# A list scheduler's cross-engine latency raised from 520 to 580 in a transformer-layer kernel

## The chip, the cores and the metric

The kernel runs on all 8 cores of one Trainium2 chip. Each core computes one of 8 sequences of 4096 tokens by itself; no data passes between cores. The metric is the device time of the slowest core in microseconds (us), the median of several runs. A matmul engine instruction is written PE, the vector engine DVE, the scalar engine ACT, GpSimd POOL, and SyncE SP.

## The reference, cut to what matters

The layer is linear attention with rotary embedding followed by a matrix product with the signs of a weight, both behind a layer norm and with a residual. D is 1024, there are 16 heads of 64.

```python
x = x + attn(layernorm(x), Wq, Wk, Wv, Wo)
x = x + einsum('bsi,oi->bso', layernorm(x), sign(weight))

# attn, per head:
q, k = phi(rope(x @ Wq.T)), phi(rope(x @ Wk.T)); v = x @ Wv.T      # phi(x) = elu(x) + 1
# scan over tokens t:
K_sum += k_t;  KV += outer(k_t, v_t)
y_t = (q_t @ KV) / max(q_t . K_sum, 1e-6)
# all heads' y side by side, then @ Wo.T
```

## The kernel before, in words

A core works through its sequence in 32 chunks of 128 tokens. The scan is done by chunk: inside a chunk a masked 128x128 product per head (L596, masked by DVE at L602 into Asb), between chunks a running sum kv in PSUM (L610) that ACT copies to KVs (L619 to L623). Each chunk has a front part (layer norm, transposes into ln1T, the products with wq, wk, wv, rope and phi, transposes into qT and kT) and a back part (attention, product with wo, residual x2, second layer norm, product with wf, residual, store). The loop at L716 mixes the back of chunk c with the front of chunk c+1.

Every product with a weight is `emit_proj` (L463): 64 matmuls of 128x128 with a sum over eight, the first 32 into one PSUM bank, the last 32 into another. When a bank is complete, it is read by ACT (qev and kev at L484, vaug at L555) or by DVE (x2 at L680 after wo, outb at L696 after wf). The banks att, pjA, pjB and pjC are handed out in turn, so the names in a row change from chunk to chunk. Of wo's two banks the one with the first half of the columns is called bank 0 here, the other bank 1. DVE adds the residual from bank 0 first (one L680), then from bank 1 (the other L680). All transposes of a chunk share one PSUM tile, ptr: L422 (ln1 and ln2), L437 (qphi, kphi) and L660 (Ysb, whose copy by ACT, L668, is the YT that wo multiplies).

No order is written by hand. Every instruction is recorded with an estimated cost and the instructions it depends on; `schedule` then runs a list scheduling for all engines, and each engine executes its instructions in the order that comes out, with semaphore waits where the data come from another engine. Two places in `schedule` use the constant `LAT`: the priority of an instruction is its cost plus the longest path behind it, with `LAT` for each edge (L80), and an instruction on another engine may start `LAT` after its producer ends (L111). An instruction is picked by earliest start, then priority (L99).

Of the kernel before, what the change touches and what calls it, by code (L numbers as in the profile page):

```python
# [28 lines left out]
class Sched:  # L29
# [34 lines left out]
    def schedule(self):  # L64
        ops = self.ops
        n = len(ops)
        succ = [[] for _ in range(n)]
        pend = [0] * n
        for op in ops:
            for d in op["deps"]:  # L70
                succ[d].append(op["i"])
                pend[op["i"]] += 1
        LAT = float(os.environ.get("SIMLAT", 520.0))
        prio = [0.0] * n
        for i in range(n - 1, -1, -1):
            m = 0.0
            for sj in succ[i]:
                if prio[sj] > m:
                    m = prio[sj]
            prio[i] = ops[i]["cost"] + (LAT if succ[i] else 0.0) + m  # L80
        eng_free = {e: 0.0 for e in ENGINES}
        avail = [0.0] * n
        done = [0.0] * n
        ready = {e: [] for e in ENGINES}
        for i in range(n):
            if pend[i] == 0:
                ready[ops[i]["engine"]].append(i)
        order = []
        remaining = n
        while remaining:  # L90
            best = None
            for e in ENGINES:
                lst = ready[e]
                if not lst:
                    continue
                ef = eng_free[e]
                for i in lst:
                    st = ef if ef > avail[i] else avail[i]
                    key = (st, -prio[i], i)  # L99
                    if best is None or key < best[0]:  # L100
                        best = (key, e, i)
            key, e, i = best
            st = key[0]
            ready[e].remove(i)
            done[i] = st + ops[i]["cost"]
            eng_free[e] = done[i]
            order.append(i)
            remaining -= 1
            for sj in succ[i]:
                pend[sj] -= 1  # L110
                t = done[i] + (LAT if ops[sj]["engine"] != e else 0.0)  # L111
                if avail[sj] < t:
                    avail[sj] = t
                if pend[sj] == 0:
                    ready[ops[sj]["engine"]].append(sj)
        cnt = {e: 0 for e in ENGINES}
        for i in order:
            ops[i]["eidx"] = cnt[ops[i]["engine"]]
            cnt[ops[i]["engine"]] += 1
        self.sim_makespan = max(done) if n else 0.0  # L120
        if os.environ.get('SIM_PRINT'):
            print('SIM makespan:', round(self.sim_makespan / 1000, 1), 'us')
            start_t = {i: done[i] - ops[i]["cost"] for i in range(n)}
            eng_prev = {}
            last = {e: None for e in ENGINES}
            for i in order:
                e2 = ops[i]["engine"]
                eng_prev[i] = last[e2]
                last[e2] = i
            cur = max(range(n), key=lambda i: done[i])  # L130
            from collections import Counter
            hist = Counter(); hist_t = Counter()
            while cur is not None:
                st = start_t[cur]
                nxt = None
                for d in ops[cur]["deps"]:
                    t = done[d] + (LAT if ops[d]["engine"] != ops[cur]["engine"] else 0)
                    if abs(t - st) < 1e-6:
                        nxt = d
                        break  # L140
                if nxt is None:
                    ep = eng_prev[cur]
                    if ep is not None and abs(done[ep] - st) < 1e-6:
                        nxt = ep
                import re as _re
                key = _re.sub(r"\d+", "#", ops[cur]["tag"]) or ops[cur]["engine"]
                hist[key] += 1; hist_t[key] += ops[cur]["cost"]
                cur = nxt
            print("SIM critical-path composition (count, total_us):")
            for k, v in hist.most_common(16):  # L150
                print(f"  {k:24s} n={v:5d}  t={hist_t[k]/1000:.1f}us")
        return order
# [666 lines left out]
```

How the kernel before makes its waits and increments, by code:

```python
        def emit_engine(name, eng):  # L744
            for op in by_engine[name]:
                i = op["i"]
                for (kind, tgt, val) in waits[i]:
                    if kind == "dma":
                        eng.wait_ge(dsems[tgt], 16 * val)
                    else:
                        eng.wait_ge(sems[tgt], inc_no[val])
                instr = op["fn"](eng)
                if op["dma"]:
                    k = dma_no[op["i"]]
                    instr.then_inc(dsems[(name, (k - 1) % 3)], 16)
                elif needs_inc[i] and instr is not None:
                    instr.then_inc(sems[name], 1)
            if name in ("sync", "gpsimd"):
                nq = sum(1 for op in by_engine[name] if op["dma"])
                for j in range(3):
                    m_tot = (nq - j + 2) // 3
                    if m_tot > 0:
                        eng.wait_ge(dsems[(name, j)], 16 * m_tot)
```

## Time and profile before

| what | value |
|---|---|
| median of 3 runs | 1180.21 us (1179.9 to 1181.19) |
| profiled execution, its own time | 1181.88 us |
| profiled execution, span of its slowest core | 1180.2 us |
| spans of the 8 cores | 1174.7 to 1180.2 us |
| PE, busy in the span | 885.2 us (75%) |
| DVE, busy | 664.0 us (56%) |
| ACT, busy | 536.0 us (45%) |
| POOL, busy | 159.2 us (13%) |
| DMA, mean | 40 GB/s |

The profile comes from one execution, and its rows are of the slowest core unless another is named. The span runs from the first to the last instruction of that core; the execution's own time is 1.7 us more. No engine is busy throughout: the shares say that the engines wait for each other.
### The profile page before, as it was taken

How to read it: one execution, taken by the hardware profiler on the slowest of the kernel's cores; microseconds unless marked ns; L12 is line 12 of the kernel's file. 1: busy time of each engine (PE TensorE's matmuls, PEld its weight loads, DVE VectorE, ACT ScalarE, POOL GpSimd, SP SyncE). 2: the span in 40 equal slices, each digit the busy share in tenths (PEclk: the TensorE clock that was granted, in tenths of full speed). 3: DMA queues.
4: the chain of work that ended last, by engine and by line, in shares of the span. 5: the costliest groups of instructions: out<-in, count | busy, mean ns of one | idle time of the engine just before them, and what ended most of it. 6: DMA issues, size and time to landing. Idle time of an engine off the chain costs nothing.

```text
span 1180.2 us, 33759 instructions; the slowest of 8 cores (1174.7 to 1180.2 us)
## 1 busy us (share of the span) xinstructions
PE 885.2 (75%) x13571; PEld 811.7 (69%) x13571; DVE 664.0 (56%) x1322; ACT 536.0 (45%) x1183; POOL 159.2 (13%) x139
## 2 busy tenths in 40 slices
PE   2427887788877877887787787878777888787785
PEld 1427776677777766777776677777667777776675
DVE  5134555665555566655556665555566555556652
ACT  3125444545444455454444545444454554445441
POOL 1201100111110011111011111110011111011110
PEclk9758899999999999999999999999999999999996
DMA  9890100110011011101101110110011101101000
GB/s 166 127 137 19 38 28 28 38 37 31 26 37 37 20 38 37 37 20 38 37 20 38 37 38 19 38 37 32 25 37 38 37 20 38 37 20 37 20 20 19
DMA packets 15145, 46.78 MB, mean 40 GB/s; under 512 B 1424, under 2 KB 1424, under 8 KB 14992
## 3 DMA queue, kind: packets, MB, share of 16 engines
q1 hardware_dynamic: 9504, 33.62, 7.8%
q0 software_dynamic: 5488, 11.01, 6.2%
q8 instruction: 109, 1.79, 0.6%
q14 instruction: 44, 0.36, 0.1%
HBM read 38.86 MB, written 16.78 MB: 47 GB/s over the span
## 4 chain that ended last, share of the span: by engine, by line
PE 29%; issue 23%; DVE 23%; ACT 12%; DMA 7%; POOL 3%; DVEq 1%; ACTq 0%; POOLq 0%; SPq 0%
PE att L470 6%; PE pjA L470 6%; PE pjC L470 6%; PE pjB L470 6%; DVE x L680 4%; DVE junkV L380 4%; DVE Asb L602 4%; POOL rB L502 3%; DMA wk<-wkT 3%; ACT qT L449 3%; ACT kev L484 2%; PE ptr L422 2%; DMA wf<-wfT 2%; DVE outb L696 2%; PE ptr L437 2%
## 5 line engine op out<-in xcount | busy, mean ns | idle before, releaser
L500 POOL TENSOR_TENSOR rA<-qev,tabS_s 128x512 bf16<-128x512 bf16 x32 | 37.0, 1158 | 835.8 <-ACT qev L484 742.7
L470 PE MATMUL pjC<-wo,YT 128*128 128x128 bf16 x480 | 83.0, 252 | 25.1 <-ACT YT L668 25.1
L470 PE MATMUL att<-wo,YT 128*128 128x128 bf16 x544 | 94.9, 255 | 7.4 <-ACT YT L668 7.4
L470 PE MATMUL pjA<-wo,YT 128*128 128x128 bf16 x544 | 94.0, 254 | 6.6 <-ACT YT L668 6.6
L470 PE MATMUL att<-wv,ln1T 128*128 128x128 bf16 x512 | 71.4, 223 | 20.3 <-ACT kev L484 13.2
L470 PE MATMUL pjB<-wo,YT 128*128 128x128 bf16 x480 | 82.3, 251 | 5.7 <-ACT YT L668 5.7
L470 PE MATMUL pjA<-wv,ln1T 128*128 128x128 bf16 x512 | 71.0, 222 | 15.4 <-ACT kev L484 15.4
L470 PE MATMUL pjC<-wv,ln1T 128*128 128x128 bf16 x512 | 70.6, 219 | 15.6 <-ACT kev L484 15.6
L470 PE MATMUL pjB<-wv,ln1T 128*128 128x128 bf16 x512 | 70.2, 219 | 15.0 <-ACT kev L484 15.0
L470 PE MATMUL pjB<-wf,ln2T 128*128 128x128 bf16 x512 | 78.1, 223 | 2.1 <-ACT ln2T L428 2.1
L470 PE MATMUL pjC<-wf,ln2T 128*128 128x128 bf16 x512 | 77.3, 223 | 1.6 <-ACT ln2T L428 1.6
L470 PE MATMUL pjA<-wf,ln2T 128*128 128x128 bf16 x512 | 77.4, 219 | 1.4 <-ACT ln2T L428 1.4
L470 PE MATMUL att<-wf,ln2T 128*128 128x128 bf16 x512 | 77.0, 219 | 1.3 <-ACT ln2T L428 1.3
L470 PE MATMUL att<-wq,ln1T 128*128 128x128 bf16 x512 | 72.4, 223 | 6.5 <-DMA wq<-wqT 6.5
L619 ACT CAST KVs<-kv 64x455 bf16<-64x455 f32 x31 | 16.5, 533 | 127.1 <-PE kv L610 127.1
L470 PE MATMUL pjA<-wq,ln1T 128*128 128x128 bf16 x512 | 72.5, 224 | 0.0
L470 PEld LDWEIGHTS pjC<-wo,YT 128*128 128x128 bf16 x480 | 52.9, 116 | 26.1 <-issue 26.1
L470 PE MATMUL pjB<-wq,ln1T 128*128 128x128 bf16 x512 | 70.3, 220 | 0.0
L470 PE MATMUL pjC<-wq,ln1T 128*128 128x128 bf16 x512 | 70.0, 219 | 0.0
L680 DVE TENSOR_TENSOR x<-pjC,xs 128x512 f32<-128x512 f32 x15 | 10.4, 692 | 104.2 <-PE pjC L470 103.0
L422 PE MATMUL ptr<-ident_s,ln 128*128 128x128 bf16 x512 | 53.7, 267 | 19.3 <-DVE ln L415 18.9
L470 PEld LDWEIGHTS att<-wo,YT 128*128 128x128 bf16 x544 | 60.9, 118 | 8.6 <-issue 8.6
(152 smaller groups left out, 2987.3 us busy)
## 6 DMA issues: line engine op xcount, KB each, us to landing
xs<-x SPq DMA_DIRECT2D x32, 512.0 KB, 3.9
out<-outb SPq DMA_DIRECT2D x32, 512.0 KB, 2.6
wq<-wqT POOLq DMA_DIRECT2D x1, 2048.0 KB, 21.9
wk<-wkT POOLq DMA_DIRECT2D x1, 2048.0 KB, 34.2
wv<-wvT POOLq DMA_DIRECT2D x1, 2048.0 KB, 47.2
wo<-woT POOLq DMA_DIRECT2D x1, 2048.0 KB, 19.4
wf<-wfT POOLq DMA_DIRECT2D x1, 2048.0 KB, 26.7
tabS_s<-tabS POOLq DMA_DIRECT2D x1, 256.0 KB, 27.9
```

The costliest lines, as they stand in the source:

```text
L380: s.add("vector", lambda e: e.tensor_scalar(out=junkV[sti][:], in0=x_sb[:], scalar1=-1.0 / D, scalar2=0.0, op0=ALU.mult, op1=ALU.add, accu ...
L422: s.add("tensor", lambda e, i=i: e.transpose(ptr[:, i * 128:(i + 1) * 128], src_sb[:, i * 128:(i + 1) * 128], ident[:]), reads=[src_res, " ...
L437: s.add("tensor", lambda e, i=i: e.transpose(ptr[:, i * 128:(i + 1) * 128], src_sb[:, i * 128:(i + 1) * 128], ident[:]), reads=[src_res, " ...
L449: s.add("scalar", lambda e, a0=a0, a1=a1: e.copy(dv[:, a0:a1, 0, :], pv[0:64, a0:a1, :]), reads=[rres], writes=[wres], tag=f"ev_{tag}e{hb} ...
L470: s.add("tensor", lambda e, o=o, i=i, pj=pj, off=off, lsb=lsb, w_sb=w_sb: e.matmul(pj[:, off:off + 128], lsb[:, i * 128:(i + 1) * 128], w_ ...
L484: s.add("scalar", lambda e, half=half, pj=pj, dst_sb=dst_sb: e.copy(dst_sb[:, half * 512:(half + 1) * 512], pj[:]), reads=[pjres], writes= ...
L500: s.add("gpsimd", lambda e: e.tensor_tensor(out=rAv, in0=HI, in1=Sb, op=ALU.mult), reads=[src_res, "tabS"], writes=["rA"], tag=f"{tag}_rA")
L502: s.add("gpsimd", lambda e: e.tensor_tensor(out=rBv, in0=LO, in1=Sb, op=ALU.mult), reads=[src_res, "tabS"], writes=["rB"], tag=f"{tag}_rB")
L602: s.add("vector", lambda e, g=g, ab=ab: e.tensor_tensor(out=Asb[:, g * 512:(g + 1) * 512].rearrange("p (h t) -> p h t", t=128), in0=ab[:, ...
L619: s.add("scalar", lambda e, kvv=kvv: e.copy(kvv[0:64, 0:455], kv[0][0:64, :]), reads=["kv0"], writes=[kvres_w], tag=f"kvev{c}_0", cost=550)
L680: s.add("vector", lambda e, half=half, pj=pj, x2sb=x2sb, x_sb=x_sb: e.tensor_tensor(out=x2sb[:, half * 512:(half + 1) * 512], in0=pj[:], i ...
L696: s.add("vector", lambda e, half=half, pj=pj, osb=osb, x2sb=x2sb: e.tensor_tensor(out=osb[:, half * 512:(half + 1) * 512], in0=pj[:], in1= ...
```

## The change

One number: the latency between engines that the scheduler reckons with goes from 520 to 580 ns.

```diff
-        LAT = float(os.environ.get("SIMLAT", 520.0))
+        LAT = float(os.environ.get("SIMLAT", 580.0))
```

The instructions are the same, and on DVE, ACT, POOL and SP they stand in the same order. Only PE's order differs, and no PE instruction moves far. The chunks in the middle of the program are alike, apart from the names of the banks, in either kernel, so one chunk shows what moved. Three places follow.

PE, the end of wo's product, where wk begins (in this chunk wo's bank 0 is pjB and bank 1 is pjC). Before:

```order
L470 MATMUL pjC<-wo,YT 128x128
L470 MATMUL pjB<-wo,YT 128x128
L470 MATMUL pjC<-wo,YT 128x128 x3
L470 MATMUL att<-wk,ln1T 128x128 x13
L470 MATMUL pjA<-wk,ln1T 128x128 x11
```

With the change:

```order
L470 MATMUL pjC<-wo,YT 128x128
L470 MATMUL pjB<-wo,YT 128x128
L470 MATMUL pjC<-wo,YT 128x128 x2
L470 MATMUL att<-wk,ln1T 128x128 x13
L470 MATMUL pjA<-wk,ln1T 128x128 x11
```

The last matmul into pjB had three matmuls into pjC behind it and has two now: bank 0 is complete one matmul later, bank 1 where it was. Between the same two neighbours (the YT transposes and wk) stand the same 136 instructions: wo, wq and the eight ln1 transposes. The last wq matmul into its first bank stays in its place, the one into its second bank moves two places ahead.

PE, around the transposes of kphi in the same chunk (the banks pjB and pjC hold wf's product here, att and pjA wv's). Before:

```order
L470 MATMUL pjB<-wf,ln2T 128x128
L470 MATMUL pjC<-wf,ln2T 128x128
L437 MATMUL ptr<-ident_s,kphi 128x128 x8
L470 MATMUL att<-wv,ln1T 128x128
L470 MATMUL pjA<-wv,ln1T 128x128
L470 MATMUL pjC<-wf,ln2T 128x128
```

With the change:

```order
L470 MATMUL pjB<-wf,ln2T 128x128
L470 MATMUL pjC<-wf,ln2T 128x128
L470 MATMUL att<-wv,ln1T 128x128
L470 MATMUL pjA<-wv,ln1T 128x128
L437 MATMUL ptr<-ident_s,kphi 128x128 x8
L470 MATMUL pjC<-wf,ln2T 128x128
```

Two wv matmuls that stood behind the eight transposes stand ahead of them. Behind the transposes 11 matmuls are left before the attention products L596, where there were 13.

PE, the same transposes in the two chunks before the last (here att and pjA hold wf's product, pjB and pjC wv's). Before:

```order
L437 MATMUL ptr<-ident_s,kphi 128x128 x7
L470 MATMUL pjB<-wv,ln1T 128x128
L470 MATMUL pjC<-wv,ln1T 128x128
L470 MATMUL att<-wf,ln2T 128x128
L470 MATMUL pjA<-wf,ln2T 128x128
L437 MATMUL ptr<-ident_s,kphi 128x128
```

With the change:

```order
L437 MATMUL ptr<-ident_s,kphi 128x128 x7
L470 MATMUL pjA<-wf,ln2T 128x128
L437 MATMUL ptr<-ident_s,kphi 128x128
```

Between the seventh transpose and the eighth stands one matmul in place of four; the other three are ahead of the first transpose.

Smaller moves, once in each chunk: the ln2 transposes come one place earlier (7 wv matmuls ahead of them, were 8), and three kv matmuls (L610) stand ahead of the first L633 where there were two, and seven at the end where there were eight. In the first chunk's front, 44 wq matmuls stand ahead of wk's first 23, where it was 46 and 25. In the last chunk, wf's product ends as wo's does: two matmuls into bank 1 behind the last into bank 0, where there were three.

## Rows read from the trace of the kernel before

**Rows 1.** The page: busy time of PE, and the chain that ended last by engine.
```profile
PE 885.2 (75%) x13571; PEld 811.7 (69%) x13571; DVE 664.0 (56%) x1322; ACT 536.0 (45%) x1183; POOL 159.2 (13%) x139
...
PE 29%; issue 23%; DVE 23%; ACT 12%; DMA 7%; POOL 3%; DVEq 1%; ACTq 0%; POOLq 0%; SPq 0%
```
**Rows 2.** Timeline of DVE, one chunk: start us, duration us, what [idle before it <-releaser].
```profile
617.32 0.69 DVE L680 TENSOR_TENSOR x<-pjB,xs 128x512 f32<-128x512 f32 x1 [10.45 <-PE pjB L470]
618.18 0.69 DVE L680 TENSOR_TENSOR x<-pjC,xs 128x512 f32<-128x512 f32 x1 [0.17 <-DVE x L680]
...
632.96 0.42 DVE L456 COPY kT<-ptr 64x512 bf16<-64x512 bf16 x1 [0.97 <-PE ptr L437]
...
633.93 0.69 DVE L696 TENSOR_TENSOR outb<-pjC,x 128x512 f32<-128x512 f32 x1
```
**Rows 3.** Timeline of PE, the same chunk.
```profile
616.99 0.22 PE L470 MATMUL pjB<-wo,YT 128*128 128x128 bf16 x1
617.04 0.33 PE L470 MATMUL pjC<-wo,YT 128*128 128x128 bf16 x3
...
632.24 0.61 PE L437 MATMUL ptr<-ident_s,kphi 128*128 128x128 bf16 x8 [1.19 <-ACT qT L452]
...
633.25 0.33 PE L470 MATMUL pjA<-wv,ln1T 128*128 128x128 bf16 x3
```
**Rows 4.** Timeline of ACT, the same chunk.
```profile
616.30 0.59 ACT L484 CAST qev<-att 128x512 bf16<-128x512 f32 x1 [5.22 <-PE att L470]
617.02 0.59 ACT L484 CAST qev<-pjA 128x512 bf16<-128x512 f32 x1
...
631.03 1.07 ACT L452 COPY qT<-ptr 64x512 bf16<-64x512 bf16 x2
```
**Rows 5.** Stretches by engine: busy us (instructions), then PEclk, DMA share, GB/s.
```profile
604.50:607.90 3.40, 1.29 (x16) 0.77 (x16) 1.95 (x7) 1.91 (x5) 0.00 (x0) 1.00 0.02 5
607.95:611.30 3.35, 3.25 (x31) 3.28 (x32) 0.00 (x0) 1.52 (x3) 0.00 (x0) 0.50 0.00 0
611.40:617.20 5.80, 5.80 (x107) 5.80 (x105) 0.00 (x0) 0.76 (x2) 0.00 (x0) 1.00 0.01 3
...
93.90:99.30 5.40, 5.38 (x51) 5.40 (x52) 0.00 (x0) 1.43 (x3) 0.00 (x0) 0.50 0.01 3
1120.60:1123.30 2.70, 2.70 (x26) 2.70 (x27) 0.00 (x0) 1.09 (x3) 0.00 (x0) 0.50 0.00 0
```
**Rows 6.** Timeline of PE, three chunks: the matmul in which the clock rises.
```profile
133.46 0.26 PE L470 MATMUL att<-wo,YT 128*128 128x128 bf16 x1
...
611.30 0.26 PE L470 MATMUL pjC<-wo,YT 128*128 128x128 bf16 x1
...
1089.13 0.28 PE L470 MATMUL att<-wo,YT 128*128 128x128 bf16 x1
```
**Rows 7.** Timeline of ACT and DVE: YT's copy in two chunks, the first residual add.
```profile
93.19 1.06 ACT L668 COPY YT<-ptr 128x512 bf16<-128x512 bf16 x2
...
607.32 1.07 ACT L668 COPY YT<-ptr 128x512 bf16<-128x512 bf16 x2 [0.99 <-PE ptr L660]
...
104.20 0.69 DVE L680 TENSOR_TENSOR x<-pjC,xs 128x512 f32<-128x512 f32 x1 [30.01 <-PE pjC L470]
```
**Rows 8.** Span and mean granted clock of two of the cores.
```profile
core 4: 1174.7 us, clock 0.926
core 5: 1180.2 us, clock 0.921
```
**Rows 9.** Timeline of PE, kphi's transposes in the second chunk before the last.
```profile
1109.98 0.55 PE L437 MATMUL ptr<-ident_s,kphi 128*128 128x128 bf16 x7 [1.19 <-ACT qT L452]
...
1110.59 0.22 PE L437 MATMUL ptr<-ident_s,kphi 128*128 128x128 bf16 x1
```
**Rows 10.** Timeline of DVE and ACT before the first wo.
```profile
53.33 1.37 DVE L504 TENSOR_TENSOR rC<-qev,tabC_s 128x512 bf16<-128x512 bf16 x1 [28.68 <-DMA tabC_s<-tabC]
...
85.49 7.03 ACT L326 ACTIVATE wf<-wf 128x8192 bf16<-128x8192 bf16 x1 [17.35 <-DMA wf<-wfT]
```

## The prediction
> **What bounds the kernel now.** I read the page first: PE is busy 75% of the span, and the chain that ended last is shared out between PE, issue time, DVE and ACT [rows 1]. So no engine sets the time; a ring of waits does, and what counts is where an instruction of the ring moves. The timeline of one chunk shows the ring. DVE sits idle for 10.45 us until wo's bank 0 is complete (its last matmul starts at 616.99), then does the first residual add at 617.32; the second add follows 0.86 later, not because of bank 1, whose last three matmuls began at 617.04, but behind the first add [rows 2, 3]. From there layer norm, rope and phi run in DVE's order, ACT copies qT until 632.10, PE does kphi's transposes at 632.24 after 1.19 us of waiting, DVE copies kT from 632.96, and masks and divides without a pause worth naming until the next YT [rows 2 to 4]. Then PE has 136 instructions in a row (wo, wq, ln1's transposes), and the ring closes.
>
> The second thing to see is TensorE's clock. Between 604.5 and 607.9 PE is busy for 1.29 of 3.40 us while DVE divides; after that the granted clock is 0.50 (1.2 GHz) from 607.95 to 611.30, while PE works at wo, and 1.00 (2.4 GHz) from 611.4 on [rows 5]. The start-to-start distance is 3.35/31 = 0.108 us in the slow stretch and 0.054 to 0.056 in the fast one [rows 3, 5]; I use 0.107 and 0.056. The rises are the point: the matmuls that straddle them stand at 133.46, 611.30 and 1089.13 [rows 6], 14 chunks apart each, and (1089.13 - 133.46)/28 = 34.13 us, (611.30 - 133.46)/14 = 34.13. Does the rise follow the work, or the work the rise? In the first chunk YT is copied at 93.19, and the rise (one period before 133.5) is at 99.4, 6.2 later; at 607.32 the distance is 4.0 [rows 5 to 7]. So it is not a fixed time after the work starts. From YT to the first add it takes 104.20 - 93.19 = 11.01 us in the one and 617.32 - 607.32 = 10.00 in the other [rows 2, 7]. 2.2 us more distance cost 1.0 us, a slope of 0.46, which is what the two rates give: a matmul done slow costs 0.107 in place of 0.056, so (0.107 - 0.056)/0.107 = 0.48 per us. That makes a lock: if the ring gets later by s against the rise, more of wo is done fast, and only 0.52 s of the delay is left at the first add. The ring's period is then the rises' 34.13 us, whatever small amount the ring itself gains or loses.
>
> Here a rule of the skill bears on it: the Trainium skill, "TensorE: Matmul & The Clock Gate", section "What's actually happening", says that the monitor's intervals run freely and are not restarted by a kernel, so that what varies is where in them a burst of matmuls falls. By that rule the rises keep their places under this change and the locked sum below holds; were the rise tied to the start of the burst instead, the unlocked sum of the rivals would. The equal distances of the rises [rows 6] beside unequal distances from YT [rows 7] agree with the rule.
>
> **The change, part by part.**
> - Bank 0 of wo is complete one matmul later, in each of 32 chunks. It lies on the path: DVE waits for it. The 136 instructions between the YT transposes and wk are the same, and by the end of wo the clock is fast, so the add starts 0.056 later than it would. With the lock, the shift at the first add in chunk n is s(n) = 0.52 s(n-1) + 0.056, which settles at 0.056/0.48 = 0.117 us after some five chunks and does not grow. Without the lock it would be 32 x 0.056 = 1.79 us.
> - wq's second bank is complete two places earlier. Nothing: the second qev copy starts 0.72 after the first [rows 4], behind it, and the first hasn't moved.
> - ln2's transposes one place earlier, kv matmuls in another order: hidden. They stand where DVE masks and divides back to back; cover gone, one place costs 0.056 a chunk, and the lock would eat that as well.
> - kphi's transposes two places later in 29 chunks. Hidden on both sides: PE has waited 1.19 us there for ACT [rows 3], which holds 2 x 0.056 = 0.11 with ease. Nor is the shorter tail behind them a gain: the tail's last matmuls start at 633.25 and end by 633.6, while outb's second half, which needs it, is taken up by DVE at 633.93 behind the kT copies [rows 2, 3].
> - kphi's transposes in two late chunks. The eight started at 1109.98 after the same wait, and the eighth came at 1110.59, 11 places later [rows 9]. With the change it is 8 places behind, and DVE's first kT copy waits for it: 3 x 0.056 = 0.167 us earlier, twice, on the path.
> - The start. DVE's first rope instruction waits for a table until 53.33, and the first wo stands behind ACT's sign of wf, which waits for its load and takes 7.03 us from 85.49 [rows 10]. Two wq matmuls moved near 40 us reach neither: 0. Were they on the path they would cost about 2 x 0.107 = 0.2.
>
> The sum, on the profiled execution: +0.117 at the first add of chunk 30; minus 0.167 at the kphi transposes makes -0.050; the next add 0.52 x -0.050 + 0.056 = +0.030; minus 0.167 makes -0.137; the last chunk's add -0.071 + 0.056 = -0.015; wf's bank 0, also one matmul later, 0.52 x -0.015 + 0.056 = +0.05 us. The last wf matmuls run as wo's do, slow first and then fast. So 1181.88 becomes 1181.9. The median of the runs is 1180.21, 1.7 below the profiled execution; the same step there gives 1180.3. That the runs differ by 1.3 us, and cores 4 and 5 by 5.5 [rows 8], with one program, I put down to where the rises fall for each; the change moves none of them.
>
> **The rivals.**
> - No lock: each chunk passes its 0.056 on. 1.79 + 0.06 for the last wf bank - 0.33 = +1.5, so 1181.7. For it: the row of DVE's wait ends on exactly this matmul. Against it: the slope of 0.46. A price of the skill would make it dearer: "TensorE: Matmul & The Clock Gate", section "Back-to-back issue gap", gives some 81 ns for each sustained matmul of 128 columns, which would make this case an estimated 33 x 0.081 - 6 x 0.081 = +2.2 us; rows 3 and 5 have 54 to 56 ns, and they decide.
> - A missed rise, the case on the slower side. The lock makes the ring start 0.12 us later against the rise. The slow part of wo is 5.4 us long in the first chunk, about 3.35 in the middle, and 2.7 near the end [rows 5]; where it starts too late for one rise, the core gets a later one. The place is wo's start in an early chunk or the one at 1120.6, where it starts latest. The price, from the longest and the shortest of these rows, is 5.4 - 2.7 = 2.7 us, which stays because the ring then hangs on the later rises: 1180.3 + 2.7 = 1183.0. It decides once the slowest core's slow part must be less than 2.7; a shift of 0.12 hardly goes there, and late in the program the 0.167 gained works against it.
> - The shorter tail counts: if the outb and vaug copies behind the kphi transposes set the pace, 2 x 0.056 x 29 = 3.2 us are saved: 1177.0. Against it stand the 0.3 us between the tail's end and DVE's taking it up [rows 2, 3], and the lock, which would give 0.1 back at most.
>
> **How the numbers follow.** A measurement of this kernel tells about 0.2%, 2.4 us, from no change. The locked case has 0.78 and its own range is that of the runs before, widened a little: 1179.2 to 1181.7. No lock has 0.11, and it too stays within 0.2%. A missed rise has 0.07, the shorter tail 0.04. Faster by over 0.2%: 0.04, and 0.01 for what I don't see. Slower: 0.07 and 0.01. Within: 0.87. The range takes in the first two cases and stops short of the other two: 1178.9 to 1182.2.
>
> **What would show it.** In the changed kernel's trace, rises 34.13 us apart as before; in a middle chunk YT's copy about 0.11 us nearer to the rise (3.9 in place of 4.0 us), and YT to first add still near 10.0; only two matmuls into bank 1 behind the last into bank 0, and the add 0.33 us after the start of that last one; PE's wait at kphi's transposes near 1.1 us in place of 1.19. Wrong would be: chunks 34.19 us apart, which means no lock; a slow stretch of wo longer than in the chunk before it, in mid program, which means a missed rise; DVE's kT copies starting sooner after ACT's qT copies, which means a gain that I have called hidden.

## The result and the profile after

The changed kernel takes 1191.64 us, the median of 8 runs from 1191.08 to 1192.75; the kernel before took 1181.3 in the same measurement. The ratio is 1.009, with a 95% interval of 1.0079 to 1.0102: slower by 0.9%, where I had forecast no change (1180.3) and a range up to 1182.2. The profiled execution of the changed kernel took 1191.08. In a few executions, whichever the kernel, the cores of a die run at a lower granted clock and take over 1% longer (one of the eight of before, 1197.05 us); the ratios leave these out, the medians count them.

The page of the changed kernel, with its line of busy times, the granted clock in 40 slices, and the chain that ended last:

```profile
PE 896.9 (75%) x13571; PEld 821.6 (69%) x13571; DVE 665.0 (56%) x1322; ACT 535.9 (45%) x1183; POOL 159.3 (13%) x139
...
PEclk9858997899999998989999999999979899999996
...
PE 31%; DVE 23%; issue 22%; ACT 12%; DMA 7%; POOL 3%; DVEq 1%; ACTq 0%; POOLq 0%; SPq 0%
```

Against [rows 1] the same number of matmuls keeps PE busy for 11.7 us more, while DVE and ACT are where they were. PE's own matmuls have become longer, which a lower clock does. The mean granted clock is lower on every core, but the cores don't lose alike; two of them, with span and mean granted clock:

```profile
core 4: 1189.4 us, clock 0.907
core 5: 1180.1 us, clock 0.914
```

Core 5 is where it was and core 4 is 14.7 us longer [rows 8]. Over the eight cores the mean span goes from 1177.3 to 1185.6, +8.4. A loss that one core has in full and another hardly at all isn't a fixed price per chunk. So I looked for the chunks in which core 4 loses it. These are the stretches of core 4 between the changes of its granted clock, with the last 3.3 us ahead of a fall cut off as a row of its own (busy us and instructions of PE, PEld, DVE, ACT, POOL; then PEclk, DMA share, GB/s):

```profile
439.70:443.00 3.30, 2.90 (x28) 2.93 (x29) 0.00 (x0) 1.69 (x4) 0.00 (x0) 0.50 0.02 5
443.10:463.50 20.40, 17.68 (x307) 17.03 (x304) 12.79 (x23) 11.16 (x28) 4.73 (x4) 1.00 0.09 28
463.60:466.90 3.30, 1.60 (x23) 1.33 (x24) 2.20 (x5) 1.81 (x4) 0.00 (x0) 1.00 0.00 0
467.00:480.50 13.50, 11.98 (x120) 10.22 (x120) 5.50 (x15) 3.47 (x7) 0.00 (x0) 0.50 0.10 40
480.70:501.00 20.30, 17.01 (x294) 16.29 (x293) 13.22 (x23) 11.86 (x28) 4.82 (x4) 1.00 0.09 29
501.10:504.40 3.30, 1.90 (x29) 1.37 (x25) 3.03 (x7) 1.18 (x2) 0.00 (x0) 1.00 0.23 96
504.60:514.60 10.00, 8.76 (x91) 7.49 (x92) 3.96 (x12) 3.47 (x7) 0.00 (x0) 0.50 0.04 15
514.80:545.40 30.60, 23.35 (x387) 21.09 (x384) 20.31 (x41) 15.02 (x35) 4.82 (x4) 1.00 0.10 36
```

The first row is the normal slow stretch at wo's start, and the last a normal fast one, which lasts until the next wo. Between them the clock falls early twice. It falls at 467.0, in the middle of attention and not at wo, and stays at 0.50 (1.2 GHz) for 13.65 us, through the division and most of the next wo. A chunk later it falls at 504.5 for 10.2 us, and then the rhythm is back. The rises stand at 443.06, 480.61 and 514.74, 37.55 and 34.13 apart. So this episode has moved the ring from one rise to a later one, and has cost 37.55 - 34.13 = 3.42 us for good.

Core 4 of the kernel before, the same part of a chunk in its own rhythm (it rises at 469.39):

```profile
469.40:489.80 20.40, 17.67 (x304) 16.91 (x302) 12.87 (x23) 11.40 (x28) 4.81 (x4) 1.00 0.09 29
489.90:493.20 3.30, 1.98 (x29) 1.67 (x29) 2.11 (x5) 1.54 (x3) 0.00 (x0) 1.00 0.00 0
493.30:500.00 6.70, 4.26 (x65) 3.14 (x64) 5.14 (x14) 1.78 (x4) 0.00 (x0) 1.00 0.19 78
500.20:503.50 3.30, 3.22 (x31) 3.25 (x32) 0.00 (x0) 1.50 (x3) 0.00 (x0) 0.50 0.02 5
```

What PE did in the 3.3 us from about 20.5 us after the rise differs: 1.98 us busy with 29 matmuls before, where the clock held, and 1.60 us with 23 after, where it fell. The timeline of PE shows what is missing. Core 4 after the change, from kphi's transposes to the second group of attention products:

```profile
464.38 0.61 PE L437 MATMUL ptr<-ident_s,kphi 128*128 128x128 bf16 x8 [1.08 <-ACT qT L452]
...
465.27 0.33 PE L470 MATMUL att<-wv,ln1T 128*128 128x128 bf16 x3
466.19 0.38 PE L596 MATMUL pjA<-qT,kT 96*128 96x128 bf16 x4 [0.58 <-DVE kT L459]
466.91 0.47 PE L596 MATMUL pjB<-qT,kT 96*128 96x128 bf16 x3 [0.34 <-DVE outb L696]
```

The same before the change:

```profile
490.41 0.61 PE L437 MATMUL ptr<-ident_s,kphi 128*128 128x128 bf16 x8 [1.19 <-ACT qT L452]
...
491.41 0.33 PE L470 MATMUL pjA<-wv,ln1T 128*128 128x128 bf16 x3
492.21 0.38 PE L596 MATMUL pjB<-qT,kT 96*128 96x128 bf16 x4 [0.47 <-DVE kT L459]
492.94 0.38 PE L596 MATMUL pjC<-qT,kT 96*128 96x128 bf16 x4 [0.34 <-DVE outb L696]
```

The wait for ACT is 0.11 shorter and the one for DVE's kT is 0.11 longer: two matmuls have crossed from behind the first wait to ahead of it, and no wait is longer in sum. The stretch between is poorer by them, and the chunk also stands later against the clock: the transposes start 464.38 - 443.06 = 21.32 us after the rise, against 490.41 - 469.39 = 21.02.

Counted in the clock records of all eight cores between 100 and 1100 us, the kernel before has no slow stretch over 11 us, and the changed one has 19 of 13.65 us, called early falls from here on: one to four on each core, five of them between 464 and 467 us. Each comes with a second, of 10.2 us, in the next chunk. (A lone slow stretch of 10.2 us near 120 us, after which the rises stand where they would, is not counted: the kernel before has it on two cores, the changed one on four.) 19 x 3.42 / 8 = 8.1 us for a mean core, of the +8.4 found. In the 19 chunks where an episode begins, kphi's transposes start 21.17 to 21.35 us after the rise, and none of the 190 other chunks whose clock held until the division has them later than 21.16. The kernel before has 17 chunks that stand as late, 21.17 to 21.33, and its clock holds in all of them; its median is 20.95. So neither the late place nor the moved transposes are enough alone: an early fall takes both.

### The profile page after: what moved, and what is told of

It reads as the page before. It is cut to its first block, busy times and chain, and to the rows that moved or that the text cites. A ratio compares the mean times of both kernels' runs of the same rounds, so it can differ in the third digit from the quotient of the medians.

```text
span 1189.4 us, 33759 instructions; the slowest of 8 cores (1180.1 to 1189.4 us)
## 1 busy us (share of the span) xinstructions
PE 896.9 (75%) x13571; PEld 821.6 (69%) x13571; DVE 665.0 (56%) x1322; ACT 535.9 (45%) x1183; POOL 159.3 (13%) x139
## 4 chain that ended last, share of the span: by engine, by line
PE 31%; DVE 23%; issue 22%; ACT 12%; DMA 7%; POOL 3%; DVEq 1%; ACTq 0%; POOLq 0%; SPq 0%
PE att L470 6%; PE pjC L470 6%; PE pjA L470 6%; PE pjB L470 6%; DVE x L680 4%; DVE junkV L380 4%; DVE Asb L602 3%; POOL rB L502 3%; DMA wk<-wkT 3%; ACT qT L449 3%; ACT kev L484 3%; PE ptr L422 2%; DMA wf<-wfT 2%; DVE outb L696 2%; PE ptr L437 2%
## 5 line engine op out<-in xcount | busy, mean ns | idle before, releaser
L470 PE MATMUL pjC<-wo,YT 128*128 128x128 bf16 x480 | 87.3, 258 | 24.6 <-ACT YT L668 24.6
L470 PE MATMUL att<-wo,YT 128*128 128x128 bf16 x544 | 97.6, 257 | 7.4 <-ACT YT L668 7.4
L470 PE MATMUL pjB<-wo,YT 128*128 128x128 bf16 x480 | 85.6, 255 | 5.8 <-ACT YT L668 5.8
L470 PEld LDWEIGHTS pjC<-wo,YT 128*128 128x128 bf16 x480 | 55.6, 119 | 25.7 <-issue 25.7
L470 PEld LDWEIGHTS pjA<-wo,YT 128*128 128x128 bf16 x544 | 62.2, 117 | 7.5 <-issue 7.5
L470 PE MATMUL pjB<-wq,ln1T 128*128 128x128 bf16 x512 | 67.4, 219 | 0.0
```

Of the source, the lines that this page charges most:

```text
L470: s.add("tensor", lambda e, o=o, i=i, pj=pj, off=off, lsb=lsb, w_sb=w_sb: e.matmul(pj[:, off:off + 128], lsb[:, i * 128:(i + 1) * 128], w_ ...
```

## The experiments

The kernels e1 to e4 have PE's order of before (LAT 520) with some of the pieces taken from the order at 580; `arrange` puts them together, and its letters name the pieces: K kphi's transposes, W the stretch of wo and wq, L ln2's transposes, V the kv matmuls, S the first chunk, F the last wf. The other engines' orders are the same in both.

**e1: kphi's transposes alone.**

```diff
-        order = s.schedule()
+        order = arrange(s, "K", None)
```

> PE's order as before, with only kphi's transposes where the change puts them (two wv matmuls ahead of them that stood behind, and three in the two late chunks). Theory K (the stretch of PE work after the kphi wait has become too thin, because two matmuls moved out of it, so TensorE's clock falls before the attention and not after it in some chunks): near the changed kernel, 1187 to 1193 us, with fast stretches cut short in 2 to 4 chunks per core. Theory W (the ring stands 0.12 us later against the clock's rises, because wo's bank 0 is complete one matmul later): no change, 1180 to 1182. Theory B (both take from the same margin, and it needs the two together): 1180 to 1184, with one early fall per core at most.

Measured: 1186.91 us, ratio 1.0046 (1.0029 to 1.0063). 11 early falls on the eight cores; 11 x 3.42 / 8 = 4.7 us, and the mean span is 1181.75, 4.5 over before. One of them on core 4, the stretch ahead of the fall and the slow one:

```profile
458.70:462.00 3.30, 1.67 (x25) 1.41 (x26) 2.20 (x5) 1.74 (x4) 0.00 (x0) 1.00 0.00 0
462.10:475.50 13.40, 11.85 (x120) 10.07 (x118) 5.42 (x15) 3.48 (x7) 0.00 (x0) 0.50 0.10 40
```

So this piece makes the falls, but only half of the time of the whole change, and fewer than the 2 to 4 on each core that I had expected. They are again the late chunks: between 100 and 1100 us the 11 start kphi's transposes 21.19 to 21.42 us after the rise, and no chunk whose clock held has them later than 21.15.

**e2: the stretch of wo and wq alone, with wo's bank 0 one matmul later.**

```diff
-        order = s.schedule()
+        order = arrange(s, "W", None)
```

> PE's order as before, with only the stretch of wo, wq and ln1's transposes as the change has it (wo's bank 0 complete one matmul later, wq's second bank two places earlier). Theory K: no change, 1180 to 1182, no early falls of the clock. Theory W: near the changed kernel, 1187 to 1193. Theory B: 1180 to 1184. In all of them YT's copy comes 0.1 us nearer to the rise than before in the middle of the program.

Measured: 1181.71 us, ratio 1.0004 (0.9994 to 1.0014), no fall in attention. The term of the sum that I had priced at +0.05 us is below what can be measured, as forecast, and the shift behind it is there: YT's copy starts 3.87 us ahead of the rise, in the median over the chunks of all cores, against 3.97 before. Core 4 in the same part of a chunk:

```profile
489.40:492.70 3.30, 1.93 (x29) 1.67 (x29) 2.15 (x5) 1.59 (x3) 0.00 (x0) 1.00 0.00 0
492.80:499.50 6.70, 4.30 (x66) 3.14 (x64) 5.19 (x14) 1.73 (x4) 0.00 (x0) 1.00 0.19 78
```

It holds the 29 matmuls of before, and the clock stays at 1.00. Elsewhere in e2 kphi's transposes start up to 21.46 us after the rise, later than in any chunk of the changed kernel that fell, without a fall in attention. The late place isn't without effect, though: in the eight chunks where they start latest, 21.37 to 21.46, the clock falls 27.3 us after the rise and not 30.7, in the division ahead of wo. One of them, on core 6, the stretch ahead of the fall and the slow one:

```profile
189.30:192.60 3.30, 2.83 (x44) 2.14 (x44) 3.09 (x7) 0.00 (x0) 0.00 (x0) 1.00 0.39 159
192.70:199.40 6.70, 5.13 (x51) 4.34 (x51) 2.18 (x8) 3.22 (x7) 0.00 (x0) 0.50 0.01 2
```

The rise comes at its place, 34.13 us after the last, and so these falls cost nothing. The later place against the clock costs no time alone, but it is what this piece adds to the other: e1 has 11 falls without it, the whole change 19 with it. The two ratios, 1.0046 and 1.0004, don't add up to 1.009.

**e3: the small moves alone** (ln2's transposes, kv matmuls, first and last chunk).

```diff
-        order = s.schedule()
+        order = arrange(s, "LVSF", None)
```

> PE's order as before, with only the rest of the change: ln2's transposes one place earlier, kv's matmuls 3 and 7 in place of 2 and 8, the first chunk's wq and wk, and the end of wf in the last chunk. Theories K, W and B: no change, 1180 to 1182, no early falls. A rival R (the kv or ln2 moves thin out a stretch of PE as well): 1183 or more, with fast stretches cut short.

Measured: 1182.1 us, ratio 1.0002 (0.9991 to 1.0012), no early fall. Hidden, as forecast.

**e4: everything but kphi's transposes.**

```diff
-        order = s.schedule()
+        order = arrange(s, "WLVSF", None)
```

> PE's order as the change has it, with kphi's transposes back where they were before. Theory K: all or nearly all of the loss is gone, 1180 to 1183. Theory W: the loss stays, 1187 to 1193. Theory B: 1180 to 1184, half a margin left.

Measured: 1183.23 us, ratio 1.0011 (1.0001 to 1.0021), no slow stretch of 13.65 us. The interval just leaves out 1, and the time is just above the 1180 to 1183 that I had if the cause is kphi's transposes. In the profiled execution one core has one episode of another kind in mid program: on core 0, where kphi's transposes start 21.64 us after the rise, the clock falls at 670.06, in the division before wo, for 10.2 us, and the rises there are 37.55 us apart, as in the others. So a shift of the ring alone can now and then cost a rise too. It is a tenth of the loss; with e1 this run settles which piece the 0.9% hangs on.

**e5: the changed kernel, with four matmuls put back into the stretch.** They multiply constants into columns of a bank that nothing reads, ahead of the first attention product of each chunk, where PE waits 0.58 us. They do no work for the result.

```diff
+            for _ in range(n):
+                s.fills.append((place, deps, lambda e: e.matmul(
+                    bank[:, cols:cols + 128], ident[:], ident[:],
+                    start=False, stop=True, skip_group_check=True)))
...
+            for place, n in ((f"v{c}_o0i0", 0), (f"tr_kT{c}0", 0), (f"A{c}_h0", 4)):
+                record(place, n, kv[2], 256, "kv2")
```

`place` names the instruction that the n extra matmuls stand ahead of; `A{c}_h0` is the first attention product of chunk c.

> The changed kernel's PE order, with four extra 128x128 matmuls on constants ahead of each chunk's first attention product (L596), into unused columns of a PSUM bank; nothing reads them. They take 4 x 0.056 = 0.22 us of the 0.47 us in which PE waits there. Theory K (the clock falls early because PE does too little in the stretch around the kphi wait): the early falls go and the time comes back to 1180 to 1183 us, although work was added. A rival P (what counts is the place of the transposes in PE's order, through some wait of DVE or ACT, and the clock only follows): no change, 1188 to 1193, or slower by the added work.

Measured: 1182.06 us, ratio 1.0009 (0.9997 to 1.002), no early fall, mean span 1177.3 as before. Core 4:

```profile
460.30:463.60 3.30, 1.83 (x27) 1.54 (x27) 2.19 (x5) 1.87 (x4) 0.00 (x0) 1.00 0.00 0
463.70:470.40 6.70, 4.55 (x68) 3.31 (x68) 5.37 (x15) 1.44 (x4) 0.00 (x0) 1.00 0.21 81
```

The changed order is untouched, work is only added, and the 0.9% is gone. 53 chunks start kphi's transposes 21.17 to 21.40 us after the rise, where each such chunk of the changed kernel fell, and none falls. A theory in which the moved transposes make something wait can't give this. The transposes' place costs time through the clock and in no other way that can be measured here.

**e6: the same move, doubled.** The order of before, with kphi's transposes four places later.

```diff
+        at = seq.index(mine[0])
+        seq = [i for i in seq if i not in mine]
+        at += 4
+        seq[at:at] = mine
```

> The order before, with kphi's transposes four places later in every chunk (the change has two places). Theory K: twice the step, so early falls in more chunks than the 11 (all cores together) of two places alone, 20 or more, and 1190 to 1205 us. Rival P, or a fall that comes by chance: about the 1187 of two places.

Measured: 1214.5 us, ratio 1.029 (1.0264 to 1.0316), above my range of 1190 to 1205: right in direction, too small in size. Over the whole span there are 76 slow stretches of 13.65 us, on each core in about every third chunk; 76 x 3.42 / 8 = 32.5 us, and the mean span is 1210.0, 32.8 over before. In mid program the clock falls in attention in the chunks between them as well, for 10.2 us, and the rise comes 34.13 us after the last. Core 4, a slow stretch of 10.2 us and one of 13.65, each with the stretch ahead of it:

```profile
435.50:438.90 3.40, 1.90 (x28) 1.32 (x26) 3.13 (x7) 1.18 (x2) 0.00 (x0) 1.00 0.27 111
439.00:449.10 10.10, 8.56 (x91) 7.29 (x88) 3.85 (x12) 3.48 (x7) 0.00 (x0) 0.50 0.04 14
...
503.80:507.10 3.30, 1.58 (x23) 1.32 (x24) 2.19 (x5) 1.72 (x4) 0.00 (x0) 1.00 0.00 0
507.30:520.80 13.50, 11.88 (x120) 10.24 (x119) 5.41 (x14) 3.47 (x7) 0.00 (x0) 0.50 0.10 40
```

Four matmuls of 0.056 us, moved over a wait in which they fit with ease, cost 2.9%.

**e7 and e8: the other way.** If idle time of PE costs clock, filling it should give time back, even from the kernel before, whose clock falls once a chunk at wo [rows 5]. e7 puts 32 such matmuls a chunk into the waits for DVE's division and ACT's copy of YT; e8 adds 34 in the waits for kev, for qT and for the first kT. The first piece of code is e7's, the second what e8 adds to it.

```diff
+            for place, n in ((f"tr_YT{c}0", 4), (f"tr_YT{c}3", 12), (f"tr_YT{c}7", 4),
+                             (f"wo{c}_o0i0", 12)):
+                record(place, n, free, 0, fres)
```

```diff
+            for place, n in ((f"v{c}_o0i0", 16), (f"tr_kT{c}0", 14), (f"A{c}_h0", 4)):
+                record(place, n, kv[2], 256, "kv2")
```

> The order before, with 32 extra 128x128 matmuls on constants in each chunk, 4, 12, 4 and 12 of them, in the four waits of PE while DVE divides and ACT copies YT, into a bank that is free there; nothing reads them. If the clock falls after that stretch because PE works too little in it, it stays at 2.4 GHz through wo: a chunk loses its slow stretch (3.35 us at 0.107 per matmul, 31 matmuls, 1.6 us) and the ring runs at its own period, 32.5 us in place of 34.13; in all 31 x 1.6 = 50 us, 1130 us, less what is given back where the ring, now not locked, brings the other thin stretches (kphi's wait, kev's wait) before a fall: 1130 to 1165. If instead the matmuls are late for their waits, or the clock goes by something else: 1180 or more.

> As the kernel with 32 extra matmuls in the division, and in each chunk 16 more in the wait for kev, 14 in the wait for qT's copies ahead of kphi's transposes, and 4 ahead of the first attention product. With all thin stretches filled, no fall of the clock in mid program and chunks of 32.5 us: 1128 to 1135 us. If the falls in the other stretches don't matter, the same as the kernel with the division alone filled.

Measured: e7 1176.12 us, ratio 0.9953 (0.9936 to 0.997); e8 1157.65, ratio 0.9804 (0.9788 to 0.9819). Both faster, and both short of what I expected (1130 to 1165 and 1128 to 1135): the size was wrong. The clock now falls at another place. Core 4 of e7, around one fall:

```profile
458.50:461.90 3.40, 2.16 (x31) 1.62 (x32) 3.23 (x7) 1.06 (x2) 0.00 (x0) 1.00 0.38 154
462.00:468.70 6.70, 6.70 (x76) 6.23 (x74) 3.20 (x11) 2.27 (x5) 0.00 (x0) 0.50 0.01 2
```

And core 2 of e8:

```profile
589.40:592.70 3.30, 2.24 (x35) 1.66 (x33) 3.03 (x7) 1.17 (x2) 0.00 (x0) 1.00 0.34 137
592.80:599.60 6.80, 6.80 (x78) 6.21 (x75) 3.73 (x12) 1.82 (x5) 0.00 (x0) 0.50 0.02 6
```

In both the fall comes out of the groups of attention products, between which PE waits for kT and outb, now that the ring is no longer held in one place against the rises. In e8 these rows come again every 34.13 us from 422 to 627 on this core: a new lock, at a poorer place.

**e9: more extra matmuls, in the waits that were left.** The order of before, e7's 32 matmuls, 32 matmuls in the wait for kev, 20 ahead of kphi's transposes, and 8, 6 and 8 ahead of three of the groups of attention products.

```diff
-            for place, n in ((f"v{c}_o0i0", 16), (f"tr_kT{c}0", 14), (f"A{c}_h0", 4)):
+            for place, n in ((f"v{c}_o0i0", 32), (f"tr_kT{c}0", 20), (f"A{c}_h0", 8),
+                             (f"A{c}_h4", 6), (f"A{c}_h8", 8)):
```

> The order of before, with more extra 128x128 matmuls on constants, in every wait of PE that was still left: per chunk 32 in the wait for kev (16 in e8), 20 ahead of kphi's transposes (14), 8, 6 and 8 ahead of the groups of A at heads 0, 4 and 8 (4, 0, 0); 32 in the waits of the division and the copy as in e8. Clock theory: e8's remaining slow stretches (core 2: from 421 to 627 us one in nearly every chunk) begin right after the A groups of L596, where PE still waited 0.25 + 0.34 + 0.47 us and where it had waited 0.4 us for qT; with these filled they go, and chunks last 32.55 to 33.4 us as e8's undisturbed ones do, instead of 34.1 to 34.3: most cores at spans of 1141 to 1147, the time 1143 to 1150 (e8: 1157.65). Rival, the extra matmuls cost their own time: 40 more by 56 ns are 2.2 us a chunk where the waits left were 1.0 + 0.4 + 1.0; if they no longer fit, chunks grow and the time is 1160 or more. Second rival, something else holds the chunk at 34.1 us there (DVE or ACT): slow stretches go but the time stays 1155 to 1160.

Measured: 1133.64 us (1133.11 to 1133.73), ratio 0.9597 (0.9581 to 0.9613): 4.0% faster than the kernel before, and beyond my range of 1143 to 1150. It is the fastest version here, 4.9% under the changed kernel. From its page:

```profile
PE 1022.9 (90%) x16889; PEld 945.7 (84%) x16889; DVE 663.6 (59%) x1322; ACT 536.3 (47%) x1183; POOL 159.2 (14%) x139
...
PEclk9767999999999999999999999999999999999998
```

And two stretches of core 4 that together are nine tenths of its span:

```profile
98.20:600.00 501.80, 485.87 (x8147) 449.98 (x8144) 309.20 (x627) 252.31 (x567) 73.77 (x62) 1.00 0.10 35
600.00:1118.60 518.60, 496.31 (x8308) 458.64 (x8305) 320.26 (x643) 255.53 (x568) 74.47 (x62) 1.00 0.09 32
```

The clock is 1.00 from 98.2 to 1118.6 without a break. PE does 3318 more matmuls than before, and the kernel is 47.6 us shorter.

**e10: the same extra matmuls, in the changed order.**

```diff
-        order = arrange(s, "", put_fills)
+        order = arrange(s, "WKLVSF", put_fills)
```

> The extra matmuls of e9 in the changed order (LAT 580). If the change costs time through the clock alone, the order is worth nothing once the clock is held up: within 0.2% of e9, no slow stretch longer than e9's. Rival, the moved instructions have a price of their own beside the clock (bank 0 of wo one place later, kphi's transposes two places later): 30 chunks by 0.05 to 0.17 us are 1.5 to 5 us, 0.13 to 0.45% over e9, at equal granted clocks.

Measured: 1135.96 us, ratio 0.9616 (0.96 to 0.9632). It is 0.2% over e9, where the two cases that I had set overlap, and the profile decides: there is no early fall here, yet the chunks differ. The first residual add of three neighbouring chunks on core 4, in e9:

```profile
594.06 0.69 DVE L680 TENSOR_TENSOR x<-pjB,xs 128x512 f32<-128x512 f32 x1 [8.92 <-PE pjB L470]
...
626.60 0.69 DVE L680 TENSOR_TENSOR x<-pjC,xs 128x512 f32<-128x512 f32 x1 [8.92 <-PE pjC L470]
...
659.15 0.69 DVE L680 TENSOR_TENSOR x<-att,xs 128x512 f32<-128x512 f32 x1 [8.92 <-PE att L470]
```

In e10:

```profile
592.42 0.69 DVE L680 TENSOR_TENSOR x<-pjB,xs 128x512 f32<-128x512 f32 x1 [8.97 <-PE pjC L470]
...
625.02 0.69 DVE L680 TENSOR_TENSOR x<-pjC,xs 128x512 f32<-128x512 f32 x1 [8.97 <-PE att L470]
...
657.62 0.69 DVE L680 TENSOR_TENSOR x<-att,xs 128x512 f32<-128x512 f32 x1 [8.97 <-PE pjA L470]
```

A chunk takes (659.15 - 594.06)/2 = 32.55 us in the one and (657.62 - 592.42)/2 = 32.60 in the other, and DVE's wait for bank 0 is 0.05 longer. This is the prediction's 0.056 for the bank that is complete one matmul later. Where the clock never falls there are no rises to lock to, and the 0.056 adds up: 31 x 0.055 = 1.7 us, less the 0.33 that the prediction had for the two late chunks, makes 1.4. From the first of these adds of a core to its last it takes 1010.3 us in e9 and 1011.6 in e10, in the mean of the cores: 1.3 of the 2.3 us between the two times. The other 1.0 wasn't followed up.

## Why the prediction was wrong

- **The ring, and wo's bank 0 at +0.05 us: right.** e2 measures no time from this piece alone, and YT stands 0.10 us nearer to the rise there, where the locked sum has 0.117. In the changed kernel itself the distance is 4.0 and not the 3.9 of my forecast, since each episode puts the ring earlier again; e5, the same order without the falls, has 3.85. The lock is there: rises are 34.13 us apart in every undisturbed chunk of the changed kernel, and YT to the first add takes 9.8 to 10.1 us there. The slope shows once more in the disturbed chunks. YT to the add takes 485.45 - 474.36 = 11.09 us where the rise comes 480.61 - 474.36 = 6.25 after YT, and 449.24 - 439.37 = 9.87 where it comes 3.69 after: 1.22/2.56 = 0.48. That the lock holds back the 0.056 is shown by e2 beside e10, where there is no lock and the chunks grow by it.
- **The small moves and the start at nothing: right** (e3).
- **The step that failed is the fourth part of the change**, kphi's transposes two places later, which the sum has at nothing: "Hidden on both sides: PE has waited 1.19 us there for ACT [rows 3], which holds 2 x 0.056 = 0.11 with ease". The time is hidden, and PE's waits have the same sum. But hidden in a wait is not without effect on a resource whose speed hangs on how PE's work lies. The two matmuls left the stretch after the wait, the clock fell there, and a fall costs 3.42 us. That this step makes the falls is shown by e1, e4 and e6, and that it does so through the clock by e5. The later place of the ring, which I had at nothing but its 0.12 us, makes them more: 19 in place of e1's 11.
- **The missed rise** (a chance of 0.07, 1183.0) had the right sign and the right kind of price, that the ring hangs on later rises from then on. It had the wrong place, cause and number. I looked for it only where wo starts too late for a rise, and priced it once, at 2.7 us. It comes from a fall in attention, at 3.42 us, one to four times on each core. What I had named as its sign, a slow stretch longer than in the chunk before it in mid program, is what led to it. At the place that I had named there is a missed rise in the runs that only shift the ring: near the end of the program the rises are 37.55 us apart on two cores of e2 and on four of e4, without a measured time of their own, and on no core of the changed kernel.
- **The lock as a guard.** I took the lock to keep any small shift small. It does so for the ring's own time. It also holds the same waits at the same place against the clock, chunk after chunk, and so a shift of 0.1 us can decide for many chunks at once: e1 alone has 11 falls, and with e2's piece, which costs nothing alone, there are 19.
- **What I could have read before.** Core 5 of the kernel before has such a fall early in the program (core 7 too, at 121.9), two rows that I didn't ask for:

```profile
119.90:123.20 3.30, 2.02 (x29) 1.47 (x26) 3.03 (x7) 1.18 (x2) 0.00 (x0) 1.00 0.24 98
123.30:133.40 10.10, 8.55 (x91) 7.29 (x91) 4.00 (x12) 3.47 (x7) 0.00 (x0) 0.50 0.05 17
```

The clock falls at 123.3 out of the attention products, and rises at 133.5 at wo. It cost nothing, since the rise came at its place, but it shows that the clock of this kernel can fall at a second place. A row of it would have made a rival: a fall before attention, priced by the distance between rises.

Which chunks fall follows from where they stand. Falls come at 464 to 467 us on five cores and at 187.6 to 190.5 on four, and the kernel before is late in the same chunks: the one whose transposes start between 456 and 462 us has them 21.20 to 21.23 us after the rise on all eight cores. The only chunks of the changed kernel that stand late and don't fall so are the last ones, one on each core near 1150 us, at 21.22 to 21.30; there the pieces of the order are others, and as in the kernel before the clock falls 27.3 us after the rise.

What stays open: why the ring stands later in these chunks, in either kernel. Nor was the loss of core 4 beyond its three falls (14.7 us against 3 x 3.42 = 10.3) followed up; spans of one core differ by some us from run to run with the rise it starts on. And it wasn't tried which of e9's extra matmuls could be left out.

## What to carry to other kernels

Where matmuls run in bursts between short waits, read the granted clock by stretches before costing a move, and find every place at which it falls, on all cores: a move that is hidden in a wait still changes how dense PE's work is on either side of it. Ask also how far each chunk stands from the last rise, since the same order fell or held by 0.1 us of that here. A chunk whose length equals the distance of the clock's rises is locked to them, so small gains and losses vanish, and large ones appear where a rise is missed. If PE is not the bound, extra matmuls that nothing reads, placed in its waits, can buy the full clock: 4.0% here, against the 0.9% that the order cost.

## What the runs showed of the hardware

- Waits of 0.2 to 1.2 us between groups of matmuls are enough for the clock to fall from 2.4 to 1.2 GHz; PE stood still for no longer than that in any of the stretches ahead of a fall shown here. The Trainium skill, "TensorE: Matmul & The Clock Gate", section "A second HAM failure mode: psum-queue depth-cycling", tells of a kernel whose small idle times between groups of matmuls let the clock swing between the two rates. The rows here agree, and add what it can cost: 0.9% for two matmuls moved, 2.9% for four, and 4.0% to be had back from the kernel before.
- With all eight cores at work and PE 90% busy, matmuls of 128 columns still start 0.055 to 0.056 us apart and the granted clock reads 1.00 for over 1000 us (e9, core 4).
- In the changed kernel an early fall is followed by another in the next chunk (13.65 us slow, then 10.2), and then by none in the two chunks behind it or more. After the first the chunk stands earlier against the rises: in the 19 second chunks kphi's transposes start 19.7 to 20.1 us after the rise, in the 19 first ones 21.2 to 21.4.
